# A transformer block on one Trainium2 core: the front in pairs of rows, identity products ahead of the gram, and two rows' mean and variance by ScalarE

## What is computed

```python
def _layernorm(x, axis=-1, eps=1e-05):
    m = jnp.mean(x, axis=axis, keepdims=True)
    v = jnp.var(x, axis=axis, keepdims=True)
    return (x - m) / jnp.sqrt(v + eps)

q = jnp.transpose(x, (2, 0, 1))                        # attention among the 4 batch rows, per position
scores = jnp.einsum('lnc,lmc->lnm', q, q) / sqrt(512)
msg = jnp.einsum('lnm,lmc->lnc', softmax(scores), q)
attn = x + jnp.transpose(msg, (1, 2, 0))

h = silu(x @ Wg.T) * (x @ Wu.T)                        # Wg, Wu: 3584 x 1024, Wd: 1024 x 3584,
ffn = h @ Wd.T                                         # dequantized from NF4 codes and block maxima

x = x + attn(_layernorm(x)); x = x + ffn(_layernorm(x))
```

## Time and profile before

| | us |
|---|---|
| median of 3 runs | 1648.34 (1648.26 to 1648.47) |
| the profiled execution | 1647.51 |
| its span, first to last instruction | 1645.8 |
| TensorE busy | 1625.6 (99%) |
| VectorE busy | 1200.6 (73%) |
| ScalarE busy | 1030.9 (63%) |
| GpSimd busy | 61.8 (4%) |

### The profile page before, as it was taken

The page is one execution under the profiler, slowest core; times in us unless marked ns, Lnnn a source line. Parts: engine busy times, 40 slices in busy tenths (PEclk is TensorE's granted clock), DMA queues, the critical chain, the costliest instruction groups (busy, mean ns, idle before and its releaser), DMA issues.

```text
span 1645.8 us, 20222 instructions
## 1 busy us (share of the span) xinstructions
PE 1625.6 (99%) x7906; PEld 786.1 (48%) x7906; DVE 1200.6 (73%) x1541; ACT 1030.9 (63%) x1123; POOL 61.8 (4%) x99
## 2 busy tenths in 40 slices
PE   6999999999999999999999999999999999999999
PEld 6964444444444444444444444444444444444444
DVE  7999968576676857667686767677977667577666
ACT  5789677677767767676676767688986536252000
POOL 4271000000000000000000000000000000000000
PEclk9999999999999999999999999999999999999999
DMA  6341233232322323142232314234764444343773
GB/s 273 141 154 40 83 110 129 75 141 77 141 96 97 124 94 141 60 159 96 96 111 107 141 51 167 96 133 145 265 224 178 152 152 177 127 179 127 256 257 129
DMA packets 77183, 226.39 MB, mean 138 GB/s; under 512 B 5280, under 2 KB 20256, under 8 KB 76576
## 3 DMA queue, kind: packets, MB, share of 16 engines
q1 hardware_dynamic: 77088, 225.10, 37.9%
HBM read 156.93 MB, written 68.16 MB: 137 GB/s over the span
## 4 chain that ended last, share of the span: by engine, by line
PE 94%; DVE 4%; ACT 1%; issue 0%; POOL 0%; DMA 0%; POOLq 0%; DVEq 0%
PE ps L1677 20%; PE ps L1679 20%; PE ps L1678 20%; PE ps L1813 10%; PE ps L1814 10%; PE ps L1815 10%; PE ps L1618 2%; DVE stats L1019 1%; PE ps L1647 1%; PE ps L1656 0%; ACT codes L688 0%; PE ps L1631 0%; POOL xb L653 0%; DVE tmp L1094 0%; DVE xa L1229 0%
## 5 line engine op out<-in xcount | busy, mean ns | idle before, releaser
L688 ACT ACTIVATE codes<-codes 128x1024 f32<-128x1024 f32 (+1 forms) x672 | 708.2, 1055 | 147.9 <-DMA codes<-q_dram 134.1
L1484 DVE SCALAR_TENSOR_TENSOR xb<-ps,y_back,xb 128x512 f32<-128x512 f32 x139 | 103.1, 749 | 71.5 <-PE ps L1815 67.8
L1677 PE MATMUL ps<-xb,rw 128*128 128x512 f16 x388 | 147.1, 379 | 0.7 <-ACT gs L780 0.7
L1677 PE MATMUL ps<-xa,wg 128*128 128x512 f16 x388 | 147.1, 379 | 0.0
L1679 PE MATMUL ps<-xa,rw 128*128 128x512 f16 x388 | 147.1, 379 | 0.0
L1679 PE MATMUL ps<-xa,wg 128*128 128x512 f16 x388 | 147.1, 379 | 0.0
L1677 PE MATMUL ps<-xa,rw 128*128 128x512 f16 x388 | 147.1, 379 | 0.0
L1678 PE MATMUL ps<-xa,rw 128*128 128x512 f16 x388 | 147.1, 379 | 0.0
L1678 PE MATMUL ps<-xb,wg 128*128 128x512 f16 x388 | 147.1, 379 | 0.0
L1678 PE MATMUL ps<-xb,rw 128*128 128x512 f16 x388 | 147.1, 379 | 0.0
L1679 PE MATMUL ps<-xb,rw 128*128 128x512 f16 x388 | 147.1, 379 | 0.0
(11 more groups left out here) (293 smaller groups left out, 2916.0 us busy)
## 6 DMA issues: line engine op xcount, KB each, us to landing
codes<-q_dram SPq DMA_DIRECT2D x84, 512.0 KB, 4.6
absm<-a_dram SPq DMA_DIRECT2D x69, 512.0 KB, 3.6
h_dram<-rw SPq DMA_DIRECT2D x28, 1024.0 KB, 4.2
gs<-h_dram SPq DMA_DIRECT2D x21, 1344.0 KB, 5.9
h_dram<-rw SPq DMA_DIRECT2D x28, 768.0 KB, 4.6
rw<-h_dram SPq DMA_DIRECT2D x11, 896.0 KB, 5.4
rw<-x_dram SPq DMA_DIRECT2D x16, 512.0 KB, 10.7
xa<-a_dram SPq DMA_DIRECT2D x13, 512.0 KB, 5.4
```

The source lines that it names most:

```text
L688: fn(real, real if step else whole, ACT.Prelu, bias=at0, scale=slope, alpha=left).then_inc(bends_done, 1)
L1484: return v.scalar_tensor_tensor(out=dst, in0=ps[:, bank, :], scalar=y_back[:, 0:1], in1=dst, op0=ALU.mult, op1=ALU.add)
L1677: mm(dst, w_hi, x_hi, start=(start and kt == 0), stop=False, skip_group_check=True)
```

## The change

**Front.** SP loads tile 0 in half rows (`load_first_x`), and tile 3 ahead of the codes. Factors are made for rows 0 and 1 as soon as those two are joined, then for rows 2 and 3, in every tile; before, that was so in tile 0 alone. Rows are written in halves throughout: ScalarE rows 0 and 1 and the second half of row 3 (in tile 0 of rows 2 and 3), GpSimd the second half of row 2, VectorE the first halves of rows 2 and 3 (in tile 0 as four quarters), with the mean subtracted and the scale multiplied, so that it need not wait for the bias. For row 3 of tiles 2 and 3 ScalarE takes the mean and the variance, in two activations with an accumulated output (`last_row_stats`), and VectorE takes three rows. TensorE runs 28 products of the identity with itself (`keep_busy`) in four portions ahead of the gram; their output is overwritten. The gram's products stand in ten pieces with waits of their own, in the same order of tiles.

**ScalarE's bends.** All stand behind tile 3 now: seven ahead of the exponential, one behind it, three between the second and the third copy, one ahead of the tenth.

**Second place.** `t_sums(0, 3)` moves behind `t_low(0, 2)`.

```diff
-            for c in range(CT - 1):
+            load_first_x()
+            for c in range(1, CT):
                 load_x(c)
             for k in range(2):
                 load_codes(k)
-            load_x(CT - 1)
...
+                if c in (2, 3) and rows.stop == B:
+                    pool.wait_ge(var_done, c - 1)
+                    g.tensor_scalar(mean_var[:, t, 3, 0:1], part_mean[:, t:t + 1], 32.0, None, ALU.mult).then_inc(p_chain, 1)
+                    chained[0] += 1
...
+            for c in range(CT):
+                norm_factors(c, 1.0, range(2), ln_first)
+                norm_factors(c, 1.0, range(2, B))
+                if c:
+                    g.tensor_scalar(y_nat[c][:, LB // 2:LB, 2, :], acc[c][:, 2, 512:1024].rearrange("p (b l) -> p b l", l=32),
+                                    ln_scale[:, c % 2, 2:3], ln_bias[:, c % 2, 2:3],
+                                    ALU.mult, ALU.add).then_inc(y_pool, 1)
...
+            def last_row_stats(c):
+
+                t, row = c % 2, acc[c][:, 3, :]
+                act.wait_ge(x_in[B * (c - 1) + 3], 16)
+                act.wait_ge(y_dve, (4, 6)[t])
+                if c == 3:
+                    act.wait_ge(var_done, 1)
+                fn(unused, row, ACT.Copy, bias=0.0, scale=1.0 / (32 * L), accum_out=part_mean[:, t:t + 1]).then_inc(mean_done, 1)
+                act.wait_ge(mean_done, c - 1)
+                fn(unused, row, ACT.Square, bias=part_mean[:, t:t + 1], scale=-1.0 / 32,
+                   accum_out=mean_var[:, t, 3, 1:2]).then_inc(var_done, 1)
+
+            def y_tile(c):
+
+                act.wait_ge(ln_first, c + 1)
+                y_halves(c, 0, range(2))
+                y_halves(c, 1, range(2))
+                if c == 2:
+                    last_row_stats(3)
+                act.wait_ge(ln_ready, c + 1)
+                y_halves(c, 1, range(3 if c else 2, B))
...
-            y_rows(CT - 1)
-            bends(0, range(4, NB))
-            bends(1, range(0, 4))
+            y_tile(0)
+            y_tile(1)
+            last_row_stats(2)
+            y_tile(2)
+            y_tile(3)
+            bends(0, range(0, 7))
             exp_half(0)
-            for k in range(10):
+            bend(0, 7)
+            copy_yt(0)
+            copy_yt(1)
+            bends(1, range(0, 3))
+            for k in range(2, 9):
                 copy_yt(k)
+            bend(1, 3)
+            copy_yt(9)
             exp_half(1)
...
             for c in range(CT):
-                for half in range(2 * B):
+                rows = B if c < 2 else 3
+                for half in range(2 * rows):
                     row_stats(c, half)
-                    if c == 0 and half == 3:
-                        row_sums(0, range(2))
-                    elif c == 1 and half == 0:
-                        y_first_halves()
-                    elif c > 1 and half == 2:
-                        y_row(c - 1)
-                row_sums(c, range(0 if c else 2, B))
-            y_row(CT - 1)
+                    if half == 3:
+                        row_sums(c, range(2))
+                    elif c and half == (0 if c == 1 else 1):
+                        y_first_halves(c - 1)
+                row_sums(c, range(2, rows))
+            y_first_halves(CT - 1)
...
             h_of_half(2)
-            t_sums(0, 3)
             x_low(26)
             x_low(27)
             t_low(0, 2)
+            t_sums(0, 3)
             x_low(28)
...
+            pe.wait_ge(consts, 5)
+            keep_busy(12)
+            pe.wait_ge(stats_ready, 2)
+            keep_busy(7)
+            pe.wait_ge(ln_first, 1)
+            keep_busy(4)
+            pe.wait_ge(stats_ready, B)
+            keep_busy(5)
+
+
+            for c, first, end, rows in ((0, 0, 8, (2, 0, 2)), (0, 8, 16, (2, 0, 4)), (0, 16, 32, (6, 0, 4)),
+                                        (1, 0, 16, (8, 0, 6)), (1, 16, 32, (11, 1, 6)),
+                                        (2, 0, 16, (13, 1, 8)), (2, 16, 24, (16, 2, 8)), (3, 0, 16, (18, 2, 10)),
+                                        (2, 24, 32, (16, 2, 8)), (3, 16, 32, (21, 3, 10))):
```

More of the change, by code:

```diff
@@ L218, in block_kernel @@
         first_silu = sb("first_silu", [P, 1], F32)
+        part_mean = sb("part_mean", [P, 2], F32)
         def xn_buf(k):
@@ L234, in block_kernel @@
         absmax_in = sem("absmax_in")
-        x_in = [sem(f"x_in{j}") for j in range(CT * B)]
+        x_first = [sem(f"x_first{j}") for j in range(2 * B)]
+        x_in = [sem(f"x_in{j}") for j in range(B, CT * B)]
         codes_in = [sem(f"codes_in{t}") for t in range(2)]
@@ L415, in load_x, with load_first_x @@
                 for n in range(B):
-                    sp.dma_start(acc[c][:, n, :], x_v[ORDER[c], n]).then_inc(x_in[B * c + n], 16)
+                    sp.dma_start(acc[c][:, n, :], x_v[ORDER[c], n]).then_inc(x_in[B * (c - 1) + n], 16)
+            def load_first_x():
+                for n in range(B):
+                    for f in range(2):
+                        cols = slice(512 * f, 512 * f + 512)
+                        sp.dma_start(acc[0][:, n, cols], x_v[ORDER[0], n][:, cols]).then_inc(x_first[2 * n + f], 16)
             def store_x1(c):
@@ L1016, in row_stats @@
                 n, f = half // 2, half % 2
-                if c < CT and f == 0:
-                    dve.wait_ge(x_in[B * c + n], 16)
+                if c == 0:
+                    dve.wait_ge(x_first[half], 16)
+                elif c < CT and f == 0:
+                    dve.wait_ge(x_in[B * (c - 1) + n], 16)
                 v.bn_stats(stats[:, n, f, :], acc[c % CT][:, n, 512 * f:512 * f + 512]).then_inc(v_chain, 1)
@@ L1596, in _, with keep_busy @@
             mm = nc.tensor.matmul
-            for c, lbs in ((0, (0, LB // 2)), (0, (LB // 2, LB)), (1, (0, LB // 2)), (1, (LB // 2, LB)), (2, (0, 3 * LB // 4)), (3, (0, LB // 2)),
-                           (2, (3 * LB // 4, LB)), (3, (LB // 2, LB))):
-                if c == 0 and lbs[0] == 0:
-                    pe.wait_ge(y_act, 2)
-                    pe.wait_ge(y_dve, 2)
-                elif c == 0:
-                    pe.wait_ge(y_act, 4)
-                elif c == 1 and lbs[0] == 0:
-                    pe.wait_ge(y_act, 6)
-                    pe.wait_ge(y_pool, 1)
-                    pe.wait_ge(y_dve, 3)
-                elif c == 1:
-                    pe.wait_ge(y_act, 8)
-                    pe.wait_ge(y_pool, 2)
-                elif lbs[0] == 0:
-                    pe.wait_ge(y_act, 2 * c + 6)
-                    pe.wait_ge(y_pool, c + 1)
-                    pe.wait_ge(y_dve, c + 2)
-                for lb in range(*lbs):
+            def keep_busy(count):
+                for _ in range(count):
+                    mm(ps[:, 7, 0:P], ident[:, :], ident[:, :], start=True, stop=True)
+            pe.wait_ge(consts, 5)
[7 more added lines that the diff above has]
+            for c, first, end, rows in ((0, 0, 8, (2, 0, 2)), (0, 8, 16, (2, 0, 4)), (0, 16, 32, (6, 0, 4)),
[3 rows of a table added]
+                pe.wait_ge(y_act, rows[0])
+                if rows[1]:
+                    pe.wait_ge(y_pool, rows[1])
+                pe.wait_ge(y_dve, rows[2])
+                for lb in range(first, end):
                     cols = y_nat[c][:, lb, :, :].rearrange("p n l -> p (n l)")
```

68 lines of the change are left out of this document (26 added, 42 removed).

## The result

| | before | changed |
|---|---|---|
| median, us (19 runs each) | 1648.46 (1648.14 to 1649.23) | 1651.51 (1649.78 to 1652.63) |
| the profiled execution | 1647.51 | 1651.51 |
| its span | 1645.8 | 1649.8 |

The ratio is 1.0019, 95% interval 1.0012 to 1.0025, so the slowdown is real: 2.0 to 4.1 us. It is smaller than the 3.3 us that the prediction drew as the border of no change, a border that was too wide for 19 runs of each. The time lies in the range on record (1646.0 to 1651.7), but at its upper end: the forecast of 1649.4 was 2.1 short. Two single executions in the runs further down (one of three places, 1753.2 us at a mean clock of 0.922, and one of before, 2466.91 us at 0.656) ran in a slow state and count in no ratio.

A forecast was written before the change was run, and what follows sets the result against it. TensorE was taken to bound the kernel, busy 1625.6 of 1645.8 us. On the profiled 1647.51, -0.1 (front) and +1.2 (sums) gave 1648.6; that execution being 0.83 under the median, the forecast was 1649.4, range 1646.0 to 1651.7.

The forecast's parts named there:

- (a): Front: half-row loads bring the moments of tile 0 at 9.6 us instead of 10.10, a gain of 0.5.
- (b): Front: quarter pieces and hand-over let the first gram product start at 11.55 us instead of 12.38.
- (c): Gram start: identity products make it warm from its first product; tile 0's 32 products take 7.1 us, ending at 18.65.
- (d): Gram: VectorE's statistics hold tile 1 to 19.3 us, TensorE waits 0.65; mask at 35.7 instead of 38.21.
- (e): Behind the exponential: ScalarE's bends put the third copy at 46.45 us, before 46.54; of 2.5 us gained, 0.1 is left.
- The clock behind the new hole: Rival: TensorE's 2.7 us stillness before 47.1 drops the clock, costing 2.3: 1651.7 us; chance 0.12.
- The sums: Second place: the 1.26 us wait at 145.87 goes, but the last transpose waits for `x_low(28)`; net 1.2 us lost.
- The cover of VectorE's lateness: After the second place: VectorE's other 1.1 us of lateness fits its own 1.62 wait at 191.44, costed at nothing.
- Bends harmless: Rival: the third copy behind the exponential is not late, so the front keeps 2.5: 1647.0 us; chance 0.10.
- transposes not held: Rival at the second place: the swap gains 1.26 and does not lose 1.2: 1646.9 us; chance 0.10.
- both: Rival: the front keeps its 2.5 us and the second place gains 1.26 together: 1644.5 us, faster; chance 0.10.
- warm-up or feeding fails: Rival in the front: identity products do not hold the clock or ScalarE's statistic is late, 1.65 later: 1651.0 us; chance 0.08.

The follow-up runs named there:

- three places: Changed kernel with eight bends ahead of the exponential, the second place reordered, and the slice's first copy ahead of two bends of job 7: 1646.68 us.
- bends ahead: Changed kernel with ScalarE's first eight bends all ahead of the exponential and the later ones spread among the copies: 1648.27 us.
- sums back: Changed kernel with the four sums put back ahead of the low half of group 26: 1649.38 us.
- before with bends moved: Kernel before with only the change's new placement of ScalarE's bends: 1650.85 us.
- both places mended: Changed kernel with eight bends ahead of the exponential, and the sums between the low halves of groups 26 and 27, low products later: 1647.05 us.
- two fills: Changed kernel with nine identity products, or 19 transposes, between TensorE's fourth and fifth transpose groups: 1650.75 and 1650.89 us.
- before, second place alone: Kernel before with only the reordered second place and the slice's first copy ahead of two bends of job 7: 1648.52 us.

## Why the forecast was 2.1 short

**(a) First statistics: wrong, mis-sized.** The moments of tile 0 were put at 9.6 and came at 10.71, later than before. The first half did land early (VectorE starts at 3.52; 3.75 was taken), but VectorE then waited for nearly each next half. The step assumed 410 GB/s for half rows; in this profile they moved at 288. The term was a gain of 0.5 and measured a loss of 0.6. The rate is not the whole cause, since the changed front with whole rows is only 0.1 earlier in the mean of three profiles.

**(b) First gram product: right in size.** 2.02 us behind the moments, 1.95 was worked out.

**(c) Clock at the start: right.** Quick from the first record; the run without the identity products shows the cause.

**(d) Tile 1 late: right.** A wait of 0.41, not 0.65; ScalarE's statistics take 1.06 and 1.15 and a read of 0.19 each, where 1.1 each was taken, and TensorE did not wait for them. The mask came at 36.95 instead of 35.7, the 1.1 of (a) carried on and some 0.1 more.

**(e) Third copy: the mechanism right.** From the exponential to it 5.2 us against 5.6. It came at 47.31 for 46.45 because the mask was late, so "0.1 left" became 0.75 lost. The run with the bends ahead shows that the place of the bends (1.9, from 46.03 to 47.94) costs more than all that the front gains (1.2, from 47.19 to 46.03).

**The clock behind the new hole: the rival that came true.** It had 0.12, and its 1651.7 is nearly the time that was measured, in part by luck: it took 2.3 for the clock, where 1.4 was measured in the profile, and the losses that it left out (0.85 and 0.4, below) made up the rest. The clock fell in four profiles with the front's 2.26 us of stillness and not in a fifth; with the other place, 17 of 19 executions of the changed kernel show a fall. Two errors stood behind the small chance. "No row shows a hole of between 1.3 and 12 us" was taken as a reason to leave it unlikely, where it only meant that nothing was known. And the second hole, 2.5 us by the prediction's own count, was not asked the same question at all.

**The sums: right.** 1.26 gone, a wait of 2.57 in its place, net 1.30 against 1.2. VectorE's lateness behind them was right too: 2.27 on top of TensorE's 2.14 (156.24 against 151.83), 2.3 in the text.

**The cover of VectorE's lateness: wrong, small.** It was costed at nothing against the slack of the earlier trace rows. VectorE's own wait did shrink (1.62 to 1.03), and by it VectorE was as late as TensorE again. But ScalarE takes sums from VectorE ahead of that wait: its activation at 188.98 stood at 184.92 before, 4.06 earlier, and its copy at 199.80 came just as late. TensorE, 3.44 late, waited 0.39 for it.

Together 0.85 (a and e) + 1.4 + 0.1 + 0.4 + 0.2 in small pieces is the 2.9 between the forecast's 1648.6 and 1651.51 in the profiled executions. In the medians it is only 2.1, and that is luck too: the sum added 0.8 because the profiled execution of before lay under its median, but the changed kernel's lies at its median. That the median of before pays more for the slow start than its profiled execution would explain this (2.3 there, 3.0 in two others); no run shows it. *Bends harmless*, *transposes not held* and *both* are out by the waits of 2.26 and 2.57; *warm-up or feeding fails* by the gram's pace.

What stays open: why the clock falls behind a hole of the same length in one execution and not in another; whether half rows are slower for their size or for the eight issues of SP, which the runs don't separate; and what keeps the moments of the changed front late even with whole rows.

## What to carry to other kernels

A gain on the engine that bounds the kernel is kept only if each engine that hands it work was moved up too: here the lead was lost at the first copy behind the gram, then at a slice's first copy, then at its second, and each time a few free operations of ScalarE stood ahead of the one that was waited for. Put such filler behind the next hand-over, and look at the whole row of hand-overs at once rather than at one. Ask of every new hole of over 2 us on TensorE what the clock does behind it, and price it by the chance of a fall, not only by its length.

## What the runs showed of the hardware

- The granted clock can fall behind 2.3 to 2.6 us of stillness, and does so in some executions only: eight of ten with the front's hole alone (sums back), four of ten with the second alone (bends ahead). It fell while TensorE still stood (before with bends moved, 0.79 from 49 to 50 us) or only some 1.8 us after it had started again (changed kernel: at work from 47.94, clock 0.71 from 49.5 to 50 us). The slow stretch lasted from 3.4 to 6.8 us and cost 1.0 to 2.5 us by the profiles. Behind 1.26 us of stillness no fall was seen (of the 105 executions of before beside the experiments, only that of 2466.91 us shows a mean clock below 1.000); with 1.71 us (both places mended) one execution of eleven may have had one.
- The same work in the hole, whether 18 product records or 19 transposes, kept it at 1.00 in one profile each, and no execution of the two fills shows 0.998.
- The slow start of a gram without warm-up cost 1.8 (before, second place alone), 2.3 and twice 3.0 us in four profiles.
- DMAs of 256 KB moved at 288 to 315 GB/s from 3 to 8 us, of 512 KB at 364 to 403. The Trainium skill, "DMA: Bandwidth & Descriptors", section Bandwidth, has smaller transfers further from the peak, for DMAs that GpSimd issues. These runs, with DMAs issued by SyncE, agree in the direction, though size and number of issues change together here.
